# Attention and ternary FFN block on eight cores: every PSUM eviction of heads 1 to 7's q, k and v moved to VectorE

## The reference, cut to what matters

```python
xn = layernorm(x)                                  # x: 8 x 4096 x 1024
q  = (xn @ Wq.T).reshape(b, t, 8, 256)             # 8 heads of 256
kv = xn @ Wkv_down.T                               # 64 wide latent
k  = (kv @ Wk_up.T).reshape(b, t, 8, 256)
v  = (kv @ Wv_up.T).reshape(b, t, 8, 256)
attn = softmax(q k^T / 16)                         # per head, all 4096 x 4096
att  = (attn @ v).reshape(b, t, 2048) @ Wo.T
gate = silu(bitlinear(xn, w_gate)); up = bitlinear(xn, w_up)
y = x + att + bitlinear(gate * up, w_down)         # int8 activations, ternary weights
```

## Time and profile before

| what | us |
|---|---|
| runs of the kernel before | 5517.83 and 5406.49, median 5462.16 |
| the profiled execution, its own time | 5414.81 |
| its span on the slowest core (core 1) | 5413.2 |
| spans of the eight cores | 5390.6 to 5413.2 |

### The profile page before, as it was taken

How to read it: one execution, slowest core, us unless ns; L and a number is a source line. 1 busy time by engine, 2 the same in 40 slices (tenths; PEclk the granted TensorE clock), 3 DMA queues, 4 the chain that set the end, 5 groups by cost and what they waited for, 6 DMA issues and landing times.

```text
span 5413.2 us, 91583 instructions; the slowest of 8 cores (5390.6 to 5413.2 us)
## 1 busy us (share of the span) xinstructions
PE 4208.6 (78%) x24244; PEld 2330.0 (43%) x24244; DVE 2047.3 (38%) x2753; ACT 2199.8 (41%) x3651; POOL 603.7 (11%) x517
## 2 busy tenths in 40 slices
PE   1223389798997988979889795688888888099999
PEld 1112156464564645646456463344443443044444
DVE  5545511212112121121211211599998999111111
ACT  4324456464563645646456463233333333000000
POOL 1000000000000000000000000233333333000000
PEclk7555599898898999989899897898998989599999
DMA  4564411011110111101111212211111111355554
GB/s 136 149 156 126 126 31 51 19 51 37 29 49 17 46 42 32 47 23 47 36 33 45 88 45 63 53 31 39 32 38 40 32 38 29 78 161 132 124 129 109
DMA packets 535679, 350.53 MB, mean 65 GB/s; under 512 B 441920, under 2 KB 486976, under 8 KB 535168
## 3 DMA queue, kind: packets, MB, share of 16 engines
q1 hardware_dynamic: 464736, 155.77, 12.1%
q0 software_dynamic: 31824, 92.95, 6.7%
q10 hardware_dynamic: 38608, 95.96, 5.5%
HBM read 244.61 MB, written 109.05 MB: 65 GB/s over the span
## 4 chain that ended last, share of the span: by engine, by line
PE 62%; DVE 18%; DMA 7%; issue 6%; ACT 5%; SPq 1%; DVEq 1%; ACTq 0%; POOLq 0%; POOL 0%
PE psF L760 17%; PE psF L749 16%; PE psF L1058 8%; PE psF L936 5%; PE psF L942 4%; PE psF L394 4%; DMA arC<-x 3%; PE psF L1044 3%; DVE rsc L474 2%; DVE rsc L477 2%; DVE arB L480 2%; DVE t L468 2%; PE psT L813 1%; ACT arB L775 1%; DMA woT_d<-arB 1%
## 5 line engine op out<-in xcount | busy, mean ns | idle before, releaser
L754 ACT ACTIVATE arB<-psF 128x512 bf16<-128x512 f32 x2048 | 1216.3, 597 | 745.3 <-PE psF L749 527.4
L760 PE MATMUL psF<-arB 128*128 128x257 bf16 x8192 | 1280.0, 278 | 97.7 <-ACT arB L775 89.0
L749 PE MATMUL psF<-arB 128*128 128x512 bf16 x4096 | 1239.2, 390 | 17.4 <-DVE arB L442 17.4
L760 PEld LDWEIGHTS psF<-arB 128*128 128x128 bf16 x8192 | 783.5, 99 | 540.3 <-issue 181.1
L942 PE MATMUL psF<-arB 128*128 128x512 bf16 x2048 | 493.3, 384 | 70.7 <-DMA arB<-wuT_d 70.7
L936 PE MATMUL psF<-arA,arB 128*128 128x512 bf16 x2048 | 536.6, 409 | 10.6 <-DMA arB<-xnqT_d 10.6
L956 POOL TENSOR_TENSOR arC<-arC 128x512 f32<-128x512 f32 x256 | 426.5, 1666 | 832.0 <-ACT arC L953 832.0
L1058 PE MATMUL psF<-arB,arA 128*128 128x512 bf16 x2048 | 450.6, 380 | 77.2 <-DMA arB<-wdT_d 77.2
L769 DVE RECIPROCAL smf<-psF 128x1 f32<-128x1 f32 x256 | 43.1, 168 | 1130.1 <-PE psF L760 1109.4
L948 ACT ACTIVATE arC<-psF,smf 128x512 f32<-128x512 f32 x256 | 176.0, 688 | 714.7 <-PE psF L942 621.9
L749 PEld LDWEIGHTS psF<-arB 128*128 128x128 bf16 x4096 | 408.0, 100 | 107.6 <-issue 28.5
(11 more groups left out here) (125 smaller groups left out, 3517.0 us busy)
## 6 DMA issues: line engine op xcount, KB each, us to landing
hqT_d<-p1b SPq DMA_DIRECT2D x32, 1024.0 KB, 6.2
arA<-hqT_d SPq DMA_DIRECT2D x32, 1024.0 KB, 6.9
arC<-Wg ACTq DMA_DIRECT2D x32, 512.0 KB, 6.0
arC<-x SPq DMA_DIRECT2D x32, 512.0 KB, 7.7
arC<-Wu ACTq DMA_DIRECT2D x32, 512.0 KB, 6.5
arC<-Wd ACTq DMA_DIRECT2D x32, 512.0 KB, 6.1
arC<-Wg POOLq DMA_DIRECT2D x32, 512.0 KB, 5.4
aoT_d<-arB SPq DMA_DIRECT2D x64, 256.0 KB, 2.1
```

The costliest lines, as they stand in the source:

```text
L749: p.add("tensor", lambda e, bi=bi, c=c, g=g, d2=d2: e.matmul(bank(g), kT[:, d2 * T + c * 128: d2 * T + (c + 1) * 128], qT[:, d2 * T + bi * ...
L754: p.add("scalar", lambda e, g=g, c=c: e.activation(pT[c % 3][:, :], bank(g), AF.Exp, bias=0.0, scale=ISCL), reads=[b_bank[g]], writes=[b_p ...
L760: p.add("tensor", lambda e, c=c, sub=sub: e.matmul(pv_ps(sub, 0, 257), pT[c % 3][:, sub * 128:(sub + 1) * 128], vA[:, c * 257:(c + 1) * 25 ...
```

## The change

In `emit_qgrp`, `emit_kgrp` and `emit_vchunk` the engine of the eviction is chosen by a new flag `vec`. For head 0 it is the old alternation. For heads 1 to 7 it is always true, so that all 16 + 16 + 32 evictions of a head are VectorE casts. No matmul, bank, buffer record or transfer changes.

```diff
@@ emit_kgrp; emit_qgrp and emit_vchunk are changed in the same way
             g = (1 + i6 % 5) if h == 0 else i6 % 6
+            vec = (i6 % 2 == 0) if h == 0 else True
...
-            p.add("vector" if i6 % 2 == 0 else "scalar",
+            p.add("vector" if vec else "scalar",
                   (lambda e, oc=oc, ts_=ts_, g=g: e.tensor_copy(
                       kT[:, oc * T + ts_ * 512: oc * T + (ts_ + 1) * 512], bank(g)))
-                  if i6 % 2 == 0 else
+                  if vec else
                   (lambda e, oc=oc, ts_=ts_, g=g: e.activation(
                       kT[:, oc * T + ts_ * 512: oc * T + (ts_ + 1) * 512], bank(g),
                       AF.Identity, bias=0.0, scale=1.0)),
@@ emit_vchunk
+            vec = (tk % 2 == 0) if h == 0 else True
```

More of the change, by code:

```diff
@@ L440, in emit_vchunk @@
                 reads=[b_kvT, b_wvuT], writes=[b_bank[g]])
-            p.add("vector" if tk % 2 == 0 else "scalar",
+            p.add("vector" if vec else "scalar",
                   (lambda e, tk=tk, g=g: e.tensor_copy(
                       vA[:, tk * 257: tk * 257 + 256], bank(g)[:, 0:256]))
-                  if tk % 2 == 0 else
+                  if vec else
                   (lambda e, tk=tk, g=g: e.activation(
```

## The result

| | kernel before | changed kernel |
|---|---|---|
| profiled execution, its own time, us | 5414.81 | 5423.77 |
| span of the slowest core, us | 5413.2 (core 1) | 5422.2 (core 0) |
| median of all runs, us | 5503.69 (27 runs) | 5588.12 (28 runs) |
| median of the runs at the common clock, us | 5408 (12 runs) | 5427 (12 runs) |
| ratio of the runs at the common clock | | 1.0039, 95% interval 1.0023 to 1.0055 |

What follows compares the result with a forecast made beforehand. PE bounds q; from there to the first QK matmul one chain of evictions and the memset decides. 1.94 + 0.89 = 2.83 us a head, 7 heads: 19.8 us upon 5414.8 gives 5435, range 5412 to 5490.

Steps and rivals of the forecast that it cites:

- term 1: q evictions of heads 1 to 7: casts at 0.86 us hide behind PE's 1.8 us a group, cost 0.
- term 2: From q to k: the last q cast now precedes k's first on VectorE, a later start of 0.28 us a head.
- terms 3 and 4: k casts step by 0.861 us and the memset waits for all sixteen: 1.94 us a head, 0.28 from the later start.
- term 5: v casts up to chunk 30: 30 steps of 0.425 + 0.17 take 17.85 us against 16.96, 0.89 us more a head.
- term 6: ScalarE, free from the q stage on, starts its first Exp no sooner because that waits for PE: 0.
- The sign that I had named: In the profile after, head 7's last q matmul to first QK matmul should come to 2.8 us more.
- The memset rival: Between k and v: the memset can begin with its record at 3035.31; +8 us, 5423; chance 0.08.
- The free self-wait: In k and v: VectorE's wait for itself costs nothing, casts overlap by 0.08; -54 us, 5361; chance 0.04.
- The rule quoted against the 0.17: Trainium skill on VectorE copy chains: a semaphore behind each adds nothing, against the 0.17 us gap assumed between casts.
- The clock rival: Behind v: PE's clock stays at 0.50 for the next 40 us; 225 us more, 5640, 4.1% slower; chance 0.03.
- I add to the profile's time, and keep the median's place for the upper end: Range's upper end: 20 us upon the two runs' median of 5462 is 5482, the upper gap adds 6; ended at 5490.

Runs made afterwards that it cites:

- the run with q alone: Changed kernel with only the q evictions of heads 1 to 7 all on VectorE, k and v alternating as before; one execution took 5413 us, stretch sum +1.9 us.
- the run alone: Changed kernel with only the v evictions of heads 1 to 7 all on VectorE, q and k alternating as before; shortest stretch 40.00 us, +0.96 us a head.
- the k run: Changed kernel with only the k evictions of heads 1 to 7 all on VectorE, q and v alternating as before; shortest stretch 40.70 us, +1.66 us a head.
- the two halves: Changed kernel with the memset of 8224 columns cut into two of 4112, the second waiting for the first; shortest stretch 42.15 us, 0.19 more than the changed kernel's.

## Why the prediction was right or wrong, point by point

- **q** (term 1, 0 us): right. A q group is PE's, and the run with q alone shows no longer q.
- **From q to k** (term 2, 0.28 us): right, 0.26 in the run with q alone.
- **k and memset** (terms 3 and 4, 1.94 with term 2): right. 0.26 + 1.66 = 1.92. The casts step by 0.86 as worked out from head 0, and the memset has moved from beside the sixteenth eviction to behind it.
- **v** (term 5, 0.89): 0.96 in the run alone. Steps of 0.597 instead of 0.595, and the first QK matmul waits as before.
- **ScalarE's freedom** (term 6, 0): right, Exp waits for QK.
- **The sum**: 2.83 us a head against 2.92, 19.8 us against 20.9 from the stretches and 21 from the ratio. The mechanism and the size of the change came out as reasoned, not by luck. The sign that I had named, 2.8 us more from the first k matmul to the first QK matmul of head 7, reads 3.3, because head 7 of the changed kernel holds one of the long steps and head 7 of the kernel before doesn't.
- **The memset rival** is out by the k run and the two halves. **The free self-wait** is out by every cast of the changed kernel; where the wait is really taken away a head gets 12 us shorter than the changed kernel's. The rule quoted against the 0.17 speaks of a semaphore and not of a wait, and no run here tests it as it stands. My price for that rival, 7.7 us below before, was too small (9.0 measured, 39.04 to 30.0), because I priced v at PE's 0.37 a matmul, where 0.33 a cast was measured. **The clock rival** is out: the clock is 0.90 behind v and PE's busy time there the same as before.
- **What failed** is the range, in the step "I add to the profile's time, and keep the median's place for the upper end". The term is the distance from the profile's time up to the median of all runs, which I took at 47 us from two runs. It measured 164 us: the median of 28 runs is 5588, the profiled execution 5424. For the kernel before it was no better known: on 27 runs the median is 5504, 89 us above its profile, and with that even the forecast's 20 us more gives 5524, outside a range that ended at 5490. Its size is set by the spread of the executions told of with the result, of which two runs were too small a sample; the counts there, nearly the same for both kernels, give no sign that the change has a part in it. Taken without that term, 5435 is within 8 us of the 5427 of the table, and 7 of the 8 are the profile's own place, 5415 over a median of 5408.

The direction of the change has two parts, and neither engine's busy time shows them. The kernel's own records made every eviction wait for the last one. Under that rule an alternation has no overlap to give, and which engine is used decides only 0.03 (v) to 0.06 us (k) an eviction; the one real overlap was the sixteenth k eviction beside the memset, and the change gave it up.

## What to carry to other kernels

When two engines alternate on one task, look whether their rows overlap at all; if each one's idle time is ended by the other, a coarse dependency has made them one engine, and moving work between them changes next to nothing. Split the record of the dependency first (here 2.3%), then ask which engine should do the work. And look for repeated work on that chain: a constant column that is written once needs no memset per head (here 8.8 us each).

## What the runs showed of the hardware that I had not expected

- A matmul's own row is no price for a stream of them. The rows of v matmuls that stand alone say 0.37 us; back to back they step by 0.22 to 0.23, at the same clock of 0.50. My bounds from single rows were too high by over a half.
- The memset's record leaves out 1.66 us of 8.57 (8224 columns) and 0.81 of 4.29 (4112 columns), so the missing part grew with the size in these two: about a fifth of the whole in both. It stands as idle time before the record, put down to nothing or to the last wait.
- Some heads are 0.28 to 0.37 us longer than the shortest, before four of seven (39.32 to 39.40 against 39.04), changed five; in the runs with one part a head or two by 0.63 to 0.64. Within each kernel it falls in the same heads on cores 0, 1 and 3, so it is no chance. In the changed kernel the whole of it is one step a head, 0.95 instead of 0.60 among the v casts (heads 1, 5 and 7) or 1.21 instead of 0.86 among the k casts (heads 2 and 4), at another cast each time. What lengthens that step wasn't tried and stays open.
